# Four residual layers on one NeuronCore: the conv layer's order, the first attention stack and the attention loop are rewritten

## The chip, the cores and the metric

The kernel runs on one core of one Trainium2 chip. The metric is the device time of one launch in microseconds (us). The kernel before was timed three times: 686.96 us in the median, from 685.99 to 689.05. A further execution was profiled, and all rows below are of that one.

## The reference

x is float32, (8, 256, 16, 16): 8 images, 256 channels, 256 positions. Four residual layers follow one another, each behind a group norm of 32 groups of 8 channels.

```
x = x + L0(gn(x)); x = x + L1(gn(x)); x = x + L2(gn(x)); x = x + L3(gn(x))

L0: norm = sqrt(sum_c f*f); fn = f / max(norm, 1e-12)      # f = gn(x)
    corr[r,cc] = sum_c pad(fn)[shifted by r,cc] * fn        # 25 shifts, 5 x 5
    y = relu(conv_w @ concat(f, corr) + conv_b)             # 256 <- 256 + 25
L1: 32 heads of 8 channels; q, k, v = split(x_r @ w_qkv.T + b)
    attn = softmax(q k^T, over the 8 IMAGES); out = attn v
L2: o = gamma * (x x^T)(W x) + x, image by image
L3: 8 experts, the best 2 of each token, gelu(x w1) * (x w3) @ w2
```

In L0 the correlation of two positions p and p' is the product of their unit vectors, which is the same as (f_p . f_p') / (|f_p| |f_p'|).

## The kernel before

A launch handles 2048 tokens (T), in 4 chunks (`NCH`) of 512 columns; a chunk holds 2 images. `x_res` is the residual stream, `x_hat` the normalised one, both with 128 channels on the partitions and 2 halves (`H`). Each engine has one block of code that it runs in order; semaphores tie the engines together. There is no planner: the order is written out by hand in the blocks of SyncE (L258), GpSimd (L350), ScalarE (L403), VectorE (L621) and TensorE (L968).

*Layer L0* goes round chunk by chunk (ScalarE L474 to 490, VectorE L702 to 724, TensorE L1031 to 1046). Of chunk t: `group_norm` sums statistics over groups on TensorE, `variance` (L646, VectorE), `deviation` (L419, ScalarE: ln and exp) and `second_half` (L656, VectorE) make scale and shift; `normalise` (L424, ScalarE) writes the lower half of x_hat and `second_half` the upper one. `squares_of` squares x_hat, `norms` (L985, TensorE) sums the squares over channels with a matrix of ones, `floor_of_norms` (L671) and `power` make 1/norm in `rnorm`, and `unit_vectors` (L675) multiplies x_hat by it into `work`. `gram` (L993) multiplies each tile of 128 tokens with its neighbourhood of 162, `gram_rows` (L442, ScalarE) copies the result out of PSUM, and SyncE writes it to DRAM and reads it back skewed (L278 to 286), which gives a band of shifts per token. `correlations` (L682) picks 25 of them under an edge mask, `turn_correlations` (L1016) transposes them, `turned_correlations` (L454, ScalarE) copies them out, and `conv_correlations` (L1024) adds their product to that of `conv_features` (L1007). `conv_out` (L458) is bias and relu, `add_conv` (L690) adds to x_res, and `statistics(1, ...)` begins the next layer's norm.

*q, k and v* come in 16 tiles: tile n is s = n // 4 (0 and 1: q and k of channels 0 to 127; 2 and 3: of 128 to 255) and chunk c = n % 4. TensorE (L1049) waits for all of L0, then for each tile makes a 128x512 product of q or k in PSUM bank n % 4 and 128 tokens of v. ScalarE (L501) and VectorE (L726) split q and k into three bfloat16 parts, GpSimd (L354) makes the third. SyncE stores the parts to DRAM (`store_parts`, L297), loads the first stack (head 0, i = 0) by six copies straight from SBUF (L305 to 310), then the other three stacks of the group by `load_stack` (L288) from DRAM: one DMA for q and three for k.

*Attention* runs in 8 groups of 4 heads, 16 units each; a unit is a 128 x 128 piece of scores for all 8 images. TensorE makes scores (L1074) and subtracts the maximum over the images (L1083), VectorE takes maximum (L747) and sum (L754), ScalarE exponentials, ln and inverse (L528 to 538), GpSimd multiplies the exponentials by the inverse (L363), and TensorE multiplies with v (L1097). `attention_steps` (L232) writes the steps of TensorE, VectorE and ScalarE: group 0 as straight code, groups 1 to 6 as a loop of two passes with three groups in its body, group 7 and the rest straight. GpSimd and SyncE have loops of their own, one pass a group.

L2 and L3 follow; the change touches them only where a semaphore's count is written (the waits on `gn_var` and the like, which count the calls of the group norm).

## Time and profile before

| | |
|---|---|
| median of three runs | 686.96 us (685.99 to 689.05) |
| the profiled execution | 684.06 us, span 681.9 us |
| TensorE matmul busy | 580.0 us, 85% of the span, 4548 instructions |
| VectorE busy | 476.0 us, 70% |
| GpSimd busy | 383.2 us, 56% |
| ScalarE busy | 327.6 us, 48% |
| chain of waits, by engine | GpSimd 38%, TensorE 35%, "issue" 10%, VectorE 7% |
| mean granted clock of TensorE | 0.896 of 2.4 GHz |

PE is TensorE (PEld its loads of weights), DVE VectorE, ACT ScalarE, POOL GpSimd, SP SyncE; a q behind a name is the engine's sequencer or queue. L363 is line 363 of the kernel before. The chain of waits is followed back from the last instruction: at each step to what released it. "issue" is time in which an engine waited for nothing that the profile shows. A timeline merges instructions of one line: start, duration, engine, line, output<-input, shapes, count, and in brackets the idle time ahead of it and what ended it. A view by stretches gives its bounds and length, then the busy us of five engines with their counts of instructions, the granted clock (1.00 is 2.4 GHz, 0.50 is 1.2 GHz), the mean share of the 16 DMA engines and the GB/s they moved.

### The profile page before, as it was taken

What the parts mean: (1) busy time and instruction counts of PE and PEld (TensorE: products, weight loads), DVE (VectorE), ACT (ScalarE), POOL (GpSimd) and SP (SyncE); (2) the same over time, 40 slices, a digit from 0 to 9 for tenths busy, and PEclk for the clock granted to TensorE, in tenths of its full rate; (3) what the DMA queues carried; (4) which work ended last, traced back from release to release, by engine and by line L of the source; (5) the groups of instructions that cost most, each with busy time, mean ns of one, the idle gap of its engine ahead of it and who ended that gap; (6) DMA issues with size and microseconds to landing.
All of it is one profiled execution on the core that took longest, in us unless ns stands there. A gap on an engine that the chain in (4) does not pass through costs nothing.

```text
span 681.9 us, 13628 instructions
## 1 busy us (share of the span) xinstructions
PE 580.0 (85%) x4548; PEld 367.2 (54%) x4549; DVE 476.0 (70%) x835; ACT 327.6 (48%) x707; POOL 383.2 (56%) x237
## 2 busy tenths in 40 slices
PE   3777795899999997999999999499974799999954
PEld 2444363655555554665555555278863366666633
DVE  3434575799999998699999999566558334334325
ACT  2334466467676765467667676234321133333310
POOL 1000046399999998479999999422001466666520
PEclk9777879699999999589999999789985699999985
DMA  9711115623112221112221100000002223222239
GB/s 303 295 33 32 32 70 149 254 85 104 70 63 70 70 69 68 31 47 71 67 67 60 62 29 1 1 0 1 32 32 65 64 79 95 86 86 92 72 100 309
DMA packets 30520, 56.58 MB, mean 83 GB/s; under 512 B 8362, under 2 KB 22339, under 8 KB 29443
## 3 DMA queue, kind: packets, MB, share of 16 engines
q1 hardware_dynamic: 25715, 38.97, 17.7%
q0 software_dynamic: 3744, 10.39, 4.9%
q10 hardware_dynamic: 1008, 6.49, 2.4%
q8 instruction: 37, 0.61, 0.4%
q14 instruction: 16, 0.13, 0.1%
HBM read 37.84 MB, written 17.40 MB: 81 GB/s over the span
## 4 chain that ended last, share of the span: by engine, by line
POOL 38%; PE 35%; issue 10%; DVE 7%; ACT 4%; DMA 3%; SPq 1%; POOLq 1%; ACTq 0%
POOL e_ring L363 38%; PE ps L1246 10%; PE ps L1262 5%; PE ps L989 2%; PE ps L1057 2%; PE ps L1178 2%; PE ps L1013 2%; DVE stats L639 2%; PE ps L1200 2%; PE ps L1002 1%; PE ps L1136 1%; PE ps L1191 1%; PE ps L1238 1%; SPq L340 1%; PE ps L1254 1%
## 5 line engine op out<-in xcount | busy, mean ns | idle before, releaser
L363 POOL TENSOR_TENSOR e_ring<-e_ring,x_hat 128x1024 f32<-128x1024 f32 x128 | 272.7, 2134 | 47.2 <-ACT x_hat L538 35.9
L528 ACT ACTIVATE e_ring<-ps 128x1024 f32<-128x1024 f32 x128 | 131.2, 1025 | 105.4 <-PE ps L1083 105.4
L747 DVE TENSOR_REDUCE m_bf<-ps 128x128 bf16<-128x1024 f32 x128 | 155.5, 1215 | 16.6 <-PE ps L1074 16.6
L754 DVE TENSOR_REDUCE x_hat<-e_ring 128x128 f32<-128x1024 f32 x128 | 154.8, 1210 | 6.4 <-ACT e_ring L528 6.3
L1074 PE MATMUL ps<-q_stack,k_stack 72*128 72x128 bf16 x1024 | 142.4, 325 | 13.3 <-DMA k_stack<-e_ring 9.7
L1074 PEld LDWEIGHTS ps<-q_stack,k_stack 72*128 72x128 bf16 x1024 | 106.5, 135 | 40.5 <-issue 40.1
L1083 PE MATMUL ps<-m_bf,ident_neg 128*128 128x512 bf16 x256 | 82.5, 406 | 14.1 <-DVE m_bf L747 6.7
L1097 PE MATMUL ps<-e_ring,v_slot 128*32 128x128 f32 x2048 | 87.7, 289 | 3.6 <-POOL e_ring L363 3.6
L1097 PEld LDWEIGHTS ps<-e_ring,v_slot 128*32 128x32 f32 x2048 | 50.9, 110 | 59.8 <-issue 53.4
L1246 PE MATMUL ps<-w_sb,e_ring 128*128 x156 | 75.2, 605 | 0.3 <-issue 0.3
L396 POOL DMA_INDIRECT pair_rows<-scratch,slot_y x39 | 38.5, 987 | 39.4 <-DVE scratch L951 37.6
L357 POOL TENSOR_TENSOR e_ring<-e_ring 128x512 bf16<-128x512 f32 x8 | 9.2, 1158 | 90.8 <-ACT e_ring L499 89.9
L944 DVE TENSOR_TENSOR scratch<-ps,e_ring 128x256 f32<-128x256 f32 x39 | 16.6, 424 | 59.7 <-ACT e_ring L611 59.7
L386 POOL DMA_INDIRECT e_ring<-token_rows,slot_x x39 | 37.9, 972 | 18.6 <-issue 11.6
L1083 PEld LDWEIGHTS ps<-m_bf,ident_neg 128*128 128x128 bf16 x256 | 18.6, 109 | 43.9 <-DVE m_bf L747 43.1
L538 ACT ACTIVATE x_hat<-x_hat 128x128 f32<-128x128 f32 x128 | 39.6, 309 | 4.7
L611 ACT ACTIVATE e_ring<-ps 128x256 f32<-128x256 f32 x39 | 15.0, 384 | 54.9 <-PE ps L1246 54.9
L1262 PE MATMUL ps<-w_sb,scratch 128*128 x156 | 40.3, 381 | 0.4 <-ACT scratch L616 0.4
L532 ACT ACTIVATE x_hat<-x_hat 128x128 f32<-128x128 f32 x128 | 38.5, 301 | 0.7 <-DVE x_hat L754 0.7
L1246 PEld LDWEIGHTS ps<-w_sb,e_ring 128*128 128x128 f32 x156 | 27.2, 194 | 19.9 <-issue 19.9
L606 ACT ACTIVATE e_ring<-ps 128x256 f32<-128x256 f32 x39 | 15.0, 384 | 37.3 <-PE ps L1238 37.3
L375 POOL TENSOR_TENSOR e_ring<-e_ring,tab 128x1248 bf16<-128x1248 bf16 x1 | 2.3, 2276 | 52.6 <-DVE e_ring L896 52.6
(149 smaller groups left out, 702.4 us busy)
## 6 DMA issues: line engine op xcount, KB each, us to landing
q_stack<-qk_parts SPq DMA_DIRECT2D x31, 288.0 KB
k_stack<-qk_parts SPq DMA_DIRECT2D x93, 96.0 KB
w_sb<-in_w13T_dram ACTq DMA_DIRECT2D x2, 2048.0 KB, 10.0
qk_parts<-e_ring SPq DMA_DIRECT2D x2, 1536.0 KB, 5.1
qk_parts<-scratch SPq DMA_DIRECT2D x2, 1536.0 KB, 16.3
x_res<-in_x_dram SPq DMA_DIRECT2D x8, 256.0 KB, 4.0
w_sb<-in_w2T_dram ACTq DMA_DIRECT2D x2, 1024.0 KB, 15.8
token_rows<-work SPq DMA_DIRECT2D x4, 512.0 KB, 3.0
```

Of the source, the lines that this page charges most:

```text
L363: nc.gpsimd.tensor_tensor(ev, ev, view(x_hat, CH + (u % RS) * P, [[0, BQ], [1, P], [0, 2]]), ALU.mult).then_inc(norm_done, 1)
L396: nc.gpsimd.indirect_dma_start(out=y_dram[:, :], in_=y_rows[:, k % YR], in_offset=None, out_offset=bass.IndirectOffsetOnAxis(ap=slot_y[:, ...
L528: nc.scalar.activation(e_ring[:, u % ER, :], score_banks(v), ACT.Exp).then_inc(exp_done, 1)
L532: nc.scalar.activation(s_ln[:, u % 2], s_sum[:, u % 2], ACT.Ln).then_inc(ln_done, 1)
L538: nc.scalar.activation(s_inv[:, u % RS], s_ln[:, u % 2], ACT.Exp, scale=-1.0).then_inc(r_done, 1)
L747: nc.vector.tensor_reduce(m_bf[:, u % 2], by_position(score_banks(v).rearrange("p a c -> p (a c)")), AXY, ALU.max).then_inc(max_done, 1)
L754: nc.vector.tensor_reduce(s_sum[:, u % 2], by_position(e_ring[:, u % ER, :]), AXY, ALU.add).then_inc(sum_done, 1)
L1074: last = nc.tensor.matmul(view(ps, 2 * (v % SLOT) * CH + (b // 2) * (2 * P) + b % 2, [[2, P]]), k_stack[:, i, b * N + mh * P:b * N + (mh + ...
L1083: last = nc.tensor.matmul(bank(2 * (v % SLOT) + j), ident_neg[:], view(m_bf, (u % 2) * P, [[0, BQ // 2], [1, P], [0, 2]]), start=False, st ...
L1097: last = nc.tensor.matmul(ps[32 * (b % 4):32 * (b % 4) + 32, 6, (b // 4) * N + nh * P:(b // 4) * N + (nh + 1) * P], v_slot[:, b * H + mh, ...
L1246: last = nc.tensor.matmul(bank((r + 1) % 2), x_turned[:, (r + 1) % 2, h * P:(h + 1) * P], w13_sb[:, h, bass.ds(e * (2 * C), 2 * C)], start ...
L1262: last = nc.tensor.matmul(ps[:, 6 + (r + 1) % 2, 0:C], gated_t[:, (r + 1) % 2, f * P:(f + 1) * P], w2_sb[:, f, bass.ds(e * C, C)], start=( ...
```

## The change

All of x is normalised first; the correlations are taken from x_hat and multiplied by 1/norm of the one position when the Gram rows leave PSUM (VectorE) and of the other when the turned correlations do. `rnorm` has two buffers. q and k tiles run over lower channels first, chunk by chunk (q and k of chunk 0, of chunk 1, ...), the first eight in two PSUM banks, and five of them are put between the last steps of L0. The first stack is loaded from DRAM as the others. `attention_steps` has no loop. The group norms of chunks 1 to 3 of layer L0 are one call (`variance(0, 1, 3)` and so on).

```diff
         def attention_steps(eng, step):
...
-            with eng.Fori(0, (NG - 2) // SLOT) as t:
-                for j in range(1, SLOT + 1):
-                    for u in range(UPG):
-                        step(t * (SLOT * UPG) + (j * UPG + u), j * UPG + u, u, t * SLOT + j, lambda k: True)
-            for u in range(UPG):
-                step((NG - 1) * UPG + u, (NG - 1) * UPG + u, u, NG - 1, lambda k: True)
+            for U in range(UPG, UNITS):
+                step(U, U, U % UPG, U // UPG, lambda k: True)
...
+        QK_TILES = [(s, c) for half in range(H) for c in range(NCH) for s in (2 * half, 2 * half + 1)]
+        QK_BANK = [2 + n % 2 if n < 2 * NCH else n % 4 for n in range(2 * H * NCH)]
+        TAIL_QK = ((0,), (1, 2), (3, 4))
...
# SyncE
             for s in range(2):
-                sp.wait_ge(part3, NCH * (s + 1))
+                sp.wait_ge(part3, 2 * NCH - 1 + s)
                 store_parts(0, s)
-            for a in range(PARTS):
-                rows_a = slice(a * PARTS * D, (a + 1) * PARTS * D)
-                q_src = parts[0][0:D, 0]
-                k_src = bass.AP(parts[0].tensor, 2 * H * UW + (PARTS + a) * T, [[H * ER * UW, D], [0, PARTS], [1, T]])
-                sp.dma_start(q_stack[rows_a, 0, :], q_src).then_inc(stack_in[0], 16)
-                sp.dma_start(k_stack[rows_a, 0, :], k_src).then_inc(stack_in[0], 16)
             for n in range(2):
                 sp.wait_ge(parts_out[n], 16)
-            for i in range(1, HPG):
+            for i in range(HPG):
                 load_stack(0, i)
...
# ScalarE, the new order of L0 and of the first tiles
+            inverse_norms(0)
+            deviation(0, 1, NCH - 1)
+            for c in range(1, NCH):
+                normalise(0, c)
+                squares_of(c)
+            for t in range(1, NCH):
+                inverse_norms(t)
+                if t >= 2:
+                    deviation(1, t - 2)
+                    normalise(1, t - 2)
+                conv_out(t - 1)
             act.wait_ge(consts_in, 16 * LATER)
+            deviation(1, NCH - 2)
+            normalise(1, NCH - 2)
+            for n in TAIL_QK[0] + TAIL_QK[1]:
+                qk_tile(n)
+            conv_out(NCH - 1)
+            for n in TAIL_QK[2]:
+                qk_tile(n)
+            deviation(1, NCH - 1)
+            normalise(1, NCH - 1)
+            for n in range(5, 2 * H * NCH):
+                qk_tile(n)
...
# VectorE
-            def unit_vectors(c):
...
+            def gram_rows(c):
+                dve.wait_ge(rn_done, c + 1)
...
+                for t in range(TPC):
+                    i, hb = c * TPC + t, t % 2
+                    dve.wait_ge(gram_done, i + 1)
+                    off = GST + (c % 2) * TPC * ROW + t * ROW + (0 if hb else REACH)
+                    q0 = (t // 2) * N + (P - REACH if hb else 0)
+                    nc.vector.tensor_tensor(view(scratch, off, [[1, ROW - REACH]]), ps[:, 2 + i % 2, 0:ROW - REACH],
+                                            rnorm[c % 2][:, q0:q0 + ROW - REACH], ALU.mult).then_inc(gram_row, 1)
+            def turned_correlations(d):
+                dve.wait_ge(cor_tr, d + 1)
+                nc.vector.tensor_tensor(cor_t[:, d * CH:(d + 1) * CH], ps[0:NK, 0, :], rnorm[d % 2][0:NK], ALU.mult
+                                        ).then_inc(cor_t_done, 1)
...
+            for t in range(1, NCH):
+                floor_of_norms(t)
+                if t >= 2:
+                    variance(1, t - 2)
+                correlations(t - 1)
+                if t >= 2:
+                    second_half(1, t - 2)
+                gram_rows(t)
+                turned_correlations(t - 1)
+                add_conv(t - 1)
+                statistics(1, t - 1)
+            dve.wait_ge(consts_in, 16 * LATER)
+            variance(1, NCH - 2)
+            second_half(1, NCH - 2)
+            for n in TAIL_QK[0]:
+                qk_tile(n)
+            correlations(NCH - 1)
+            turned_correlations(NCH - 1)
+            for n in TAIL_QK[1]:
+                qk_tile(n)
+            add_conv(NCH - 1)
+            statistics(1, NCH - 1)
+            for n in TAIL_QK[2]:
+                qk_tile(n)
+            variance(1, NCH - 1)
+            second_half(1, NCH - 1)
+            for n in range(5, 2 * H * NCH):
+                qk_tile(n)
...
# TensorE
+            group_norm(0, 0)
+            conv_features(0, 0)
+            norms(0)
+            group_norm(0, 1, NCH - 1)
+            gram(0)
+            conv_features(0, 1)
+            for t in range(1, NCH):
+                norms(t)
+                if t >= 2:
+                    group_norm(1, t - 2)
+                gram(t)
+                turn_correlations(t - 1)
+                conv_features(t, 0)
+                conv_correlations(t - 1)
+                conv_features(t, 1)
+            group_norm(1, NCH - 2)
+            for n in TAIL_QK[0]:
+                qk_tile(n)
+            turn_correlations(NCH - 1)
+            for n in TAIL_QK[1]:
+                qk_tile(n)
+            conv_correlations(NCH - 1)
+            for n in TAIL_QK[2]:
+                qk_tile(n)
+            group_norm(1, NCH - 1)
+            for n in range(5, 2 * H * NCH):
+                qk_tile(n)
```

`gram` reads x_hat in place of `work` and waits for x_hat alone. `qk_tile` holds what the body of the loop over 16 tiles held, with the bank from `QK_BANK`, and a tile waits for the second tile before it to have left its bank (n < 8), or the fourth.

## Rows read from the trace of the kernel before

**Rows 1.** the page's chain of waits by line, share of the span

```profile
POOL e_ring L363 38%; PE ps L1246 10%; PE ps L1262 5%; PE ps L989 2%; PE ps L1057 2%; PE ps L1178 2%; PE ps L1013 2%; DVE stats L639 2%; PE ps L1200 2%; PE ps L1002 1%; PE ps L1136 1%; PE ps L1191 1%; PE ps L1238 1%; SPq L340 1%; PE ps L1254 1%
```

**Rows 2.** timeline of GpSimd in attention: start us, us, instructions, idle before

```profile
218.44 31.48 POOL L363 TENSOR_TENSOR e_ring<-e_ring,x_hat 128x1024 f32<-128x1024 f32 x14 [0.65 <-ACT x_hat L538]
...
255.16 15.67 POOL L363 TENSOR_TENSOR e_ring<-e_ring,x_hat 128x1024 f32<-128x1024 f32 x7 [0.65 <-ACT x_hat L538]
...
275.77 2.13 POOL L363 TENSOR_TENSOR e_ring<-e_ring,x_hat 128x1024 f32<-128x1024 f32 x1 [4.95 <-ACT x_hat L538]
...
303.92 31.48 POOL L363 TENSOR_TENSOR e_ring<-e_ring,x_hat 128x1024 f32<-128x1024 f32 x14 [0.47 <-ACT x_hat L538]
```

**Rows 3.** timeline of TensorE at the seam of the loop

```profile
265.29 1.05 PE L1074 MATMUL ps<-q_stack,k_stack 72*128 72x128 bf16 x8
...
271.20 1.89 PE L1074 MATMUL ps<-q_stack,k_stack 72*128 72x128 bf16 x8 [3.58 <-issue]
```

**Rows 4.** busy us of PE, PEld, DVE, ACT, POOL; clock, DMA share, GB/s

```profile
270.00:271.00 1.00, 0.00 (x0) 0.00 (x0) 0.00 (x0) 0.00 (x0) 0.82 (x1) 0.50 0.22 86
...
292.00:294.00 2.00, 2.00 (x22) 1.28 (x22) 1.31 (x2) 1.56 (x4) 0.48 (x1) 0.53 0.01 2
```

**Rows 5.** the same view for the time ahead of attention

```profile
11.00:120.00 109.00, 82.95 (x268) 45.70 (x268) 56.14 (x159) 51.79 (x106) 18.45 (x16) 0.83 0.35 117
```

**Rows 6.** timeline of VectorE, the floors of the norms of chunks 1 and 3

```profile
29.41 0.69 DVE L673 TENSOR_SCALAR scratch<-ps 128x512 f32<-128x512 f32 x1 [5.32 <-PE ps L989]
...
65.55 0.69 DVE L673 TENSOR_SCALAR scratch<-ps 128x512 f32<-128x512 f32 x1 [5.44 <-PE ps L989]
```

**Rows 7.** SyncE, TensorE's first scores; GB/s of 95:128 us in 40 slices

```profile
98.72 5.57 SPq L299 DMA_DIRECT2D qk_parts<-e_ring  x2
...
120.71 3.57 PE L1074 MATMUL ps<-q_stack,k_stack 72*128 72x128 bf16 x16 [9.69 <-DMA k_stack<-e_ring]
...
GB/s 0 0 0 20 0 238 477 477 343 372 0 194 298 462 477 462 70 45 60 40 45 55 60 55 50 50 55 50 50 60 70 129 159 129 139 119 129 109 144 253
```

**Rows 8.** VectorE's lines ahead of attention by form: count | busy us, mean ns

```profile
L731 DVE SCALAR_TENSOR_TENSOR e_ring<-ps,qk_bias_sb,scratch 128x512 f32<-128x512 f32 x8 | 6.0, 750 | 1.8 <-ACT scratch L504 1.8
...
L735 DVE TENSOR_TENSOR work<-ps,v_bias_sb 128x256 f32<-128x256 f32 x16 | 6.6, 413 | 0.0
...
L693 DVE TENSOR_TENSOR x_res<-x_res,scratch 128x1024 f32<-128x1024 f32 x4 | 4.9, 1217 | 1.5 <-ACT scratch L465 1.5
...
L639 DVE BATCH_NORM_STATS2 stats<-x_res 128x6 f32<-128x256 f32 x32 | 11.2, 414 | 5.0 <-DMA x_res<-in_x_dram 4.9
...
L660 DVE SCALAR_TENSOR_TENSOR gn_tmp<-gn 128x4 f32<-128x4 f32 x8 | 1.3, 163 | 7.3 <-ACT gn L417 7.3
```

**Rows 9.** SyncE, first band's read; the four reads, us to landing

```profile
30.61 0.37 SPq L285 DMA_DIRECT2D scratch<-gram_rows  x1
...
scratch<-gram_rows SPq DMA_DIRECT2D x4, 138.0 KB, 2.3
```

**Rows 10.** timeline of ScalarE: ln of the norms, the last normalisation

```profile
48.31 0.63 ACT L416 ACTIVATE scratch<-scratch 128x512 f32<-128x512 f32 x1 [3.75 <-DVE scratch L673]
...
91.50 1.09 ACT L429 ACTIVATE x_hat<-x_res,gn 128x256 f32<-128x256 f32 x2 [0.82 <-DVE gn L663]
```

**Rows 11.** timeline of TensorE: features, correlations' product cold and warm

```profile
48.06 3.71 PE L1013 MATMUL ps<-x_hat,conv_wT_sb 128*128 128x512 f32 x8
...
58.27 3.73 PE L1027 MATMUL ps<-e_ring,conv_cT_sb 25*128 25x512 f32 x4 [3.42 <-ACT e_ring L456]
...
72.65 1.98 PE L1027 MATMUL ps<-e_ring,conv_cT_sb 25*128 25x512 f32 x4 [0.33 <-ACT e_ring L456]
```

**Rows 12.** timeline of GpSimd, the first eight tiles of q and k

```profile
93.83 10.08 POOL L357 TENSOR_TENSOR e_ring<-e_ring 128x512 bf16<-128x512 f32 x8 [89.94 <-ACT e_ring L499]
```

**Rows 13.** SyncE, a load of q; GB/s of 174:184 us in 40 slices

```profile
174.95 0.77 SPq L291 DMA_DIRECT2D q_stack<-qk_parts  x1
...
GB/s 98 66 82 82 49 33 16 33 0 66 49 0 49 49 115 131 131 213 131 98 115 164 82 197 147 82 82 49 82 82 66 98 49 82 16 0 0 0 0 0
```

More of the change, by code:

```diff
@@ L119, in conv_stack_kernel @@
         TPC = CH // P
-        rnorm = scratch[:, 0:CH]
-        GST = CH
+        rnorm = [scratch[:, i * CH:(i + 1) * CH] for i in range(2)]
+        GST = 2 * CH
         BAND = GST + 2 * TPC * ROW
@@ L353, in _ @@
             pool.wait_ge(pool_init, 2)
-            for n in range(2 * H * NCH):
-                s, c = n // NCH, n % NCH
+            for n, (s, c) in enumerate(QK_TILES):
                 pool.wait_ge(part2, n + 1)
@@ L1009, in conv_features @@
                     pe.wait_ge(conv_in, 16 * CONV)
+                normed(0, BPC * (d + 1) - 1)
                 if d >= 2:
```

240 lines of the change are left out of this document (92 added, 148 removed).

## The prediction

> **What bounds the kernel now.** I read the page's chain of waits first, then GpSimd's timeline through attention, then the first 121 us engine by engine, then the queue of SyncE around the first scores. The chain shows that the longest stretch hangs on one GpSimd instruction, the multiplication of the exponentials on L363: 38% of the span, and most of it is this one line [rows 1]; eight groups of sixteen units make 128 of them. They follow one another every 2.26 us (14 of them take 31.48 us, each 2.13 us long), and one group of sixteen units lasts 255.16 - 218.44 = 36.72 us [rows 2]. While GpSimd is the bound, nothing that the change does to the other engines inside attention counts, with one exception. Between the same place of two groups there are once 303.92 - 255.16 = 48.76 us, 12.04 us more than 36.72 [rows 2]. That place is the seam between the first and the second pass of the loop in the function attention_steps: GpSimd, which has a loop of its own by groups, stands still for 4.95 us, and before it TensorE for 3.58 us, on nothing that the profile shows ("issue") [rows 2, 3]. Then TensorE's granted clock is 0.50 (the 1.2 GHz level) and is still 0.53 some 22 us later [rows 4]; the eight score matmuls of a unit take 1.89 us instead of 1.05 [rows 3]. So the seam costs 12.0 us: the stall itself and the slow clock behind it.
>
> Ahead of attention no engine is full. TensorE's clock was 0.83 in the mean from 11 to 120 us, and it was busy for 83 of the 109 us [rows 5]. The chunks go round a chain through all three engines, from one floor of the norms to the next: 18 us for the last two of them, (65.55 - 29.41) / 2 [rows 6]. The first scores begin at 120.71, after 9.69 us of waiting for the first stack [rows 7].
>
> **Part 1, the straight loop.** It takes out the jump back of TensorE, VectorE and ScalarE. The 64 units ahead of the seam are straight code already, 16 before the loop and 48 in its first pass, and the two groups' starts in [rows 2] that lie there are the steady 36.72 us apart. With every unit written out I expect that pace throughout: -12.0 us. Bounds: nothing is gained if the stall is merely met elsewhere; more than 12.04 us can't be, as that is all the seam costs. I take the upper end, as it is what the row shows of straight code.
>
> The Trainium skill, on the page "Runtime: NRT & Kernel Launch", section "Instruction fetch mechanics", says that instructions are prefetched in sequence and that a taken jump to code outside the small buffer has to wait for a fetch from memory. By that rule the stall goes, as in my sum; the trace agrees with it in the 3.58 us [rows 3].
>
> **Part 2, the conv layer.** Removed: the unit vectors (one 128x1024 multiplication per chunk) from the chain, and the normalisation and squares of a chunk from between two chunks. Added: each 128x162 row copy goes from ScalarE to VectorE and becomes a product with the norms; no row has it. Its shapes lie below 128x256 (413 ns) and 128x512 (750 ns) of the same kind [rows 8]; on the line through both, 162 columns come to 0.29 us. Bounds 0.2 and 0.41 us; four per chunk, so at most 0.5 us a chunk later. The turned correlations, 512 columns, I take at 0.75 us, the nearest row, between 0.4 and 0.75.
>
> I lay the new order out by these lengths. *First chunk*: x_hat at 11.0 as before; the features, now ahead of the norms, cost what the unit vectors gave, and I put its four rows at 20.5. Normalising the rest follows in 7 us. VectorE then stands in order before the correlations of chunk 0, and these wait for the band. Its read was issued at 30.61 and such a read lands in 2.3 us [rows 9]. The write ahead of it shares the DMA engines with the weights' 6 MB, issued in the same place as before, so writing the rows a little earlier doesn't help, and the band is there at 32.9. From there: correlations, rows of chunk 1 (with TensorE cold after 5 us of idling) to 36.1, turned 37.7, features and correlations product to about 41, relu, addition, statistics (0.7 + 1.22 + 1.8 us, the last four of 414 ns [rows 8] and two small ones) to 44.8. The floor of chunk 2 is thus at 44.8 instead of 47.6.
>
> *From one floor to the next*, warm, in us after the floor begins: floor 0.7 [rows 6]; inverse norms (two of 0.63 [rows 10]) 2.0; deviation 2.45; second half (four small ones of about 0.2 with their gaps, two 128x256 of some 0.4 [rows 8]) 4.0; rows, two waiting for their Gram matmuls, 5.9; turning 6.2; turned correlations 6.95, beside them features on TensorE to 7.75 (two pairs take 3.71 [rows 11]); correlations' product 1.7 [rows 11], 9.45; relu 10.15; addition 11.4; statistics 13.2. Cold, features and product take 3.4 and 3.4 (the product 3.73 against 1.98 with its pipeline's end [rows 11]): 16.6. The transfer of the rows lies beside all this. So 13.2 to 16.6 us in place of 18.
>
> *The tail.* Behind the last statistics of chunk 2 the new order sets in one line on VectorE: group norm 3.4, tile 0 to 5.6, correlations and turned of chunk 3 to 7.25, tiles 1 and 2 to 10.4, product, relu, addition and statistics of chunk 3 to 14.45, tiles 3 and 4 (1.1 us each [rows 8]) 16.65, group norm and x_hat 19.8 (1.09 us at the end as in [rows 10]); tiles 5 to 7, and 25.9 until GpSimd has the third part of the eighth tile. TensorE idles in it for over 2 us before turning chunk 3, so cold it is 2 to 4 us more. The moved tiles hide little: correlations of chunk 3, ready since its band came, now stand behind tile 0.
>
> Sum to the eighth tile: all warm 44.8 + 13.2 + 13.2 + 25.9 = 97.1; all cold 44.8 + 33.2 + 29.5 = 107.5. It was 103.9 (93.83 + 10.08 [rows 12]). The middle is 102.3, and the mean clock of 0.83 [rows 5] lies between the two levels; I take 102.5, 1.4 us earlier. The tiles behind the eighth run at TensorE's 1.3 us as before and end 7 us later, ahead of the stack.
>
> **Part 3, the first stack by DRAM.** Six copies from SBUF go, ahead of which nothing of the stack can land; the scores began at 120.71, 16.8 us after the eighth tile [rows 7, 12]. Now the two stores of 1.57 MB leave 1.3 us apart. The first alone fills five slices of 0.825 us behind its issue at 98.72 (238 to 477 GB/s, 4.1 us) [rows 7]; both at 430 GB/s are 7.3 us, begun 0.9 us ahead of the eighth tile, so with the landing they are there 6.9 us behind it (5.7 at the best slices' rate, 7.8 at the first store's). One issue of q and three of k follow; the traffic of such a load, issued at 174.95, ends in the 35th of 40 slices of 0.25 us, at 182.9, or 8.0 us later [rows 13]. So the scores may begin 6.9 + 0.1 + 8.0 = 15.0 us after the eighth tile: -1.8 us. Bounds: 6.5 us for the load, as its tail may be that of others (-3.3), and 11 us, as three more loads follow at once (+1.2). The second stack follows by 6 us, and unit 4 needs it only some 9 us after the start. TensorE idles 8 us in either, so the cold start of attention, 8.7 us to GpSimd's first product, stays.
>
> The Trainium skill ("DMA: Bandwidth & Descriptors", the section on why a DMA increments its semaphore by 16) says that the slowest dimension of a pattern sets how many of the 16 engines share a DMA. The load of q leads with a dimension of three copies; by the rule three engines carry all 288 KB. The slices with a long tail at about 82 GB/s [rows 13] agree; by it there is no 6.5 us, and the sum would be the same 8.0.
>
> **Sum.** Scores begin at 102.5 + 15.0 = 117.5 against 120.7: -3.2. With the seam -12.0: -15.2 us. What follows attention has the same instructions in the same order. The profiled execution took 684.06 us (span 681.9 and 2.2 around it): 668.9. The median of the runs, 686.96, lies 2.9 above; from it 671.8. I say 671.5.
>
> **Rivals.** *B, the clock holds up front (0.15)*: eighth tile 97.1, scores 112.1, -8.6; with -12.0 a time of 666. For it: TensorE's longest gap in a chunk shrinks from 3.4 us [rows 11] to about 2.6. Against: the clock was 0.83 with TensorE busy for 76% of the time [rows 5], and in the new order that share hardly rises.
> *C, the new order is slower up front (0.15)*: all cold, eighth tile 107.5, scores 122.5, +1.8; 677. VectorE now carries rows, turned correlations and tiles in one order; each late band or stall holds all behind it.
> *D, one stall stays (0.05)*: if the supply of instructions stalls once in the longer straight code, it costs the 12.04 us again: 684. The seam may be a matter of distance and not of the jump. Against it speak 64 units without one.
> *E, slower (0.05)*: the same mechanism, in attention, met twice or more, since 48 more units have to be fetched by three engines while the stacks load: each stall with its slow clock is 12.04 us, so with two the time is 671.8 + 24.1 = 696. It decides from the second stall on.
> *Mine, A*: 0.60.
>
> **How the numbers follow.** About 0.5% (3.4 us) is what a measurement can tell from no change. A, B and C are faster: 0.90; D is within: 0.05; E slower: 0.05. The range leaves out D, E and the edges of B and C: 663 to 679, from -24 (B with the better stack) to -8 (C with the worse stack).
>
> **What would show it.** Right: GpSimd's products 2.26 us apart from start to end, each group 36.7 us, no clock of 0.50 inside attention; floors of chunks 2 and 3 near 44.8 and 60; the eighth tile near 102.5; scores 15 us later with TensorE waiting for a k_stack from qk_parts. Wrong: a stall on "issue" inside attention, first scores before 112 or after 123, or floors over 18 us apart. If the part behind attention changes by more than 1 us, the sum has missed something.

## The result, and the profile of the changed kernel

The changed kernel takes 679.88 us (median of 10 runs, 676.09 to 682.86) against 687.61 us of the kernel before (10 runs, 683.09 to 698.43): ratio 0.9887, 95% interval 0.9855 to 0.9920. It is 7.7 us faster, where the prediction had 15.2. Its profiled execution took 682.86 us, the longest of its ten, and the one of before 684.06, shorter than its median; so the two profiles lie only 1.2 us apart and the stages have to be compared one by one. Ratios, here and below, are estimated from fast runs alone, which leaves out runs far above the fastest of their kernel (one of the six of s2 below took 933.11 us, at a mean clock of 0.555), while the medians are of all runs.

*Attention.* GpSimd's timeline of the changed kernel, where [rows 2] shows the seam:

```profile
219.94 31.48 POOL L361 TENSOR_TENSOR e_ring<-e_ring,x_hat 128x1024 f32<-128x1024 f32 x14 [0.65 <-ACT x_hat L530]
251.77 4.23 POOL L361 TENSOR_TENSOR e_ring<-e_ring,x_hat 128x1024 f32<-128x1024 f32 x2 [0.35 <-ACT x_hat L530]
256.65 31.48 POOL L361 TENSOR_TENSOR e_ring<-e_ring,x_hat 128x1024 f32<-128x1024 f32 x14 [0.65 <-ACT x_hat L530]
288.49 4.23 POOL L361 TENSOR_TENSOR e_ring<-e_ring,x_hat 128x1024 f32<-128x1024 f32 x2 [0.36 <-ACT x_hat L530]
```

From one group's place to the next there are 256.65 - 219.94 = 36.71 us, across the former seam as everywhere else; no idle time of 4.95 us, and no clock of 0.50 from 138 us until attention ends. Its last product ends at 423.52 us, against 434.07 before: 10.55 us sooner.

*Ahead of attention.* Floors of chunks 1 to 3 on VectorE; the eighth tile on GpSimd; SyncE's stores of lower q and k and its first loads; TensorE's first scores:

```profile
25.83 0.69 DVE L667 TENSOR_SCALAR scratch<-ps 128x512 f32<-128x512 f32 x1 [2.23 <-PE ps L1008]
45.01 0.69 DVE L667 TENSOR_SCALAR scratch<-ps 128x512 f32<-128x512 f32 x1
59.89 0.68 DVE L667 TENSOR_SCALAR scratch<-ps 128x512 f32<-128x512 f32 x1
...
102.14 1.15 POOL L355 TENSOR_TENSOR e_ring<-e_ring 128x512 bf16<-128x512 f32 x1 [0.82 <-ACT e_ring L465]
...
101.34 2.33 SPq L304 DMA_DIRECT2D qk_parts<-e_ring  x2
110.68 0.91 SPq L296 DMA_DIRECT2D q_stack<-qk_parts  x1
111.64 1.42 SPq L300 DMA_DIRECT2D k_stack<-qk_parts  x2
...
120.79 3.57 PE L1106 MATMUL ps<-q_stack,k_stack 72*128 72x128 bf16 x16 [10.39 <-DMA k_stack<-qk_parts]
```

The floors are where the prediction put them (45.01 and 59.89 for 44.8 and 60; [rows 6] had 65.55 for the last). The eighth tile's third part is there at 102.14 + 1.15 = 103.29 us, 0.6 us sooner than in [rows 12], and then 17.5 us pass to the first scores (16.8 before, 15.0 in the sum): 120.79 against the 120.71 of [rows 7]. Of the 5.7 us that the last floor gained nothing is left: from that floor to the eighth tile there are 103.29 - 59.89 = 43.4 us, where the old order needed 103.91 - 65.55 = 38.4 (the prediction had 42.5).

*Start of attention.* The view by stretches, first of before and then of the changed kernel:

```profile
120.00:130.00 10.00, 9.29 (x38) 7.60 (x39) 6.02 (x6) 2.56 (x4) 0.63 (x1) 0.50 0.58 202
130.00:140.00 10.00, 8.70 (x96) 5.40 (x95) 9.83 (x10) 7.26 (x14) 9.55 (x5) 1.00 0.62 258
```

```profile
120.00:130.00 10.00, 9.21 (x38) 7.63 (x39) 5.93 (x5) 2.56 (x4) 0.55 (x1) 0.50 0.74 292
130.00:140.00 10.00, 10.00 (x72) 7.40 (x71) 8.80 (x9) 6.05 (x12) 7.96 (x4) 0.62 0.35 146
```

With the same start, TensorE is at full clock from 130 us before and gets 0.62 in the mean of 130 to 140 us now: GpSimd has 4 products behind it in that stretch instead of 5.

*Behind attention* nothing was changed, but from the end of attention to the end of the span there are 680.7 - 423.52 = 257.2 us instead of 681.9 - 434.07 = 247.8. Two stages carry it. The first lies between the addition to x_res and the product with the tables on GpSimd, 77.76 us before (443.97 to 521.73) and 81.05 now:

```profile
433.01 2.49 POOL L370 TENSOR_TENSOR x_res<-x_res,x_hat 128x512 f32<-128x512 f32 x2 [9.49 <-ACT x_hat L427]
...
514.06 2.28 POOL L373 TENSOR_TENSOR e_ring<-e_ring,tab 128x1248 bf16<-128x1248 bf16 x1 [53.43 <-DVE e_ring L916]
```

The second is the 39 expert slots, whose results GpSimd writes one by one to pair_rows: 111.65 us from the first to the last of them before (every 3.02 us in the steady part), 657.33 - 539.03 = 118.30 us now. It limps, that is, short and long steps take turns:

```profile
566.64 0.99 POOL L394 DMA_INDIRECT pair_rows<-scratch,slot_y  x1 [0.30 <-DVE scratch L958]
569.25 0.99 POOL L394 DMA_INDIRECT pair_rows<-scratch,slot_y  x1 [0.34 <-issue]
574.32 0.99 POOL L394 DMA_INDIRECT pair_rows<-scratch,slot_y  x1 [2.80 <-DVE scratch L971]
576.92 0.99 POOL L394 DMA_INDIRECT pair_rows<-scratch,slot_y  x1 [0.34 <-issue]
...
571.30 0.39 ACT L598 ACTIVATE e_ring<-ps 128x256 f32<-128x256 f32 x1 [3.24 <-remote]
```

The steps are 2.6, 5.1 and 2.6 us long, and at a long one ScalarE stood still for 3.24 us, until 571.30, though TensorE's product for it had ended at 568.67. So there were four questions: what the loop was worth, what the conv order, what the stack, and whether the part behind attention belongs to the change.

### The profile page after: what moved, and what is told of

The parts are those of the page before. It is cut to its first block, busy times and chain, and to the rows that moved or that the text cites. A ratio compares the mean times of both kernels' runs of the same rounds, so it can differ in the third digit from the quotient of the medians.

```text
span 680.7 us, 13220 instructions
## 1 busy us (share of the span) xinstructions
PE 573.0 (84%) x4540; PEld 363.3 (53%) x4541; DVE 474.5 (70%) x835; ACT 320.2 (47%) x683; POOL 383.5 (56%) x237
## 4 chain that ended last, share of the span: by engine, by line
POOL 38%; PE 32%; DVE 9%; issue 9%; DMA 4%; ACT 4%; another core or an unknown queue 1%; SPq 1%; POOLq 1%; ACTq 0%; DVEq 0%
POOL e_ring L361 38%; PE ps L1278 9%; PE ps L1294 5%; DVE stats L631 2%; PE ps L1061 2%; PE ps L1232 2%; PE ps L1210 2%; PE ps L1032 1%; PE ps L1168 1%; PE ps L1270 1%; DMA gram_rows<-scratch 1%; PE ps L1223 1%; PE ps L1286 1%; PE ps L1021 1%
## 5 line engine op out<-in xcount | busy, mean ns | idle before, releaser
L1106 PE MATMUL ps<-q_stack,k_stack 72*128 72x128 bf16 x1024 | 139.5, 320 | 10.4 <-DMA k_stack<-qk_parts 10.4
L1106 PEld LDWEIGHTS ps<-q_stack,k_stack 72*128 72x128 bf16 x1024 | 104.4, 133 | 36.9 <-issue 36.8
L1115 PE MATMUL ps<-m_bf,ident_neg 128*128 128x512 bf16 x256 | 80.4, 397 | 13.4 <-DVE m_bf L767 5.8
L1129 PE MATMUL ps<-e_ring,v_slot 128*32 128x128 f32 x2048 | 85.2, 283 | 3.6 <-POOL e_ring L361 3.6
L598 ACT ACTIVATE e_ring<-ps 128x256 f32<-128x256 f32 x39 | 15.0, 385 | 43.4 <-PE ps L1270 31.5
## 6 DMA issues: line engine op xcount, KB each, us to landing
w_sb<-in_w13T_dram ACTq DMA_DIRECT2D x2, 2048.0 KB, 10.1
w_sb<-in_w2T_dram ACTq DMA_DIRECT2D x2, 1024.0 KB, 15.7
```

The costliest lines, as they stand in the source:

```text
L1106: last = nc.tensor.matmul(view(ps, 2 * (v % SLOT) * CH + (b // 2) * (2 * P) + b % 2, [[2, P]]), k_stack[:, i, b * N + mh * P:b * N + (mh + ...
L1115: last = nc.tensor.matmul(bank(2 * (v % SLOT) + j), ident_neg[:], view(m_bf, (u % 2) * P, [[0, BQ // 2], [1, P], [0, 2]]), start=False, st ...
L1129: last = nc.tensor.matmul(ps[32 * (b % 4):32 * (b % 4) + 32, 6, (b // 4) * N + nh * P:(b // 4) * N + (nh + 1) * P], v_slot[:, b * H + mh, ...
```

## The experiments

Every ratio is to the kernel before, timed on the same chip in the same job. The jobs were r1 to r4, s1 to s4, t1 to t4, u1 to u4, v1 and v2; the kernel before had medians of 685.54, 681.91, 689.41, 685.60 and 688.57 us in them, so times of different jobs are not compared.

**First job: the parts of the change.** r1 is the changed kernel again.

> The changed kernel once more, unaltered: is the slow slot loop of its first profile (39 slots from 539.0 to 657.3 us, 118.3 us, where the kernel before needed 111.7) a property of the program or of that one execution? Theory P (the program: its longer straight code puts the slot loop elsewhere, and ScalarE stalls in it): the slot loop takes about 118 us again and the median stays near 680. Theory E (the execution): the slot loop takes about 112 us and the profiled time is near 676, the lowest of the ten runs.

r2 is the kernel before with the loop of `attention_steps` written out, and nothing else:

```diff
-            with eng.Fori(0, (NG - 2) // SLOT) as t:
-                for j in range(1, SLOT + 1): ...
-            for u in range(UPG): ...
+            for U in range(UPG, UNITS):
+                step(U, U, U % UPG, U // UPG, lambda k: True)
```

> The kernel before with the attention loop written out and nothing else. By the prediction's own step the seam's 12.0 us go: 675.5 from 687.6. Theory P: the straight code costs some 6 us in the slot loop, so about 681. Theory E: 675 to 676, and all that is missing from the forecast is the front part, which then is worth nothing or a loss.

r3 is the changed kernel with that loop put back (the same diff, read backwards).

> The changed kernel with the attention loop of before put back; conv order, tile order and the first stack stay as changed. By the prediction: 684.4, 3.2 us under the kernel before. By the two profiles (scores begin at 120.79 against 120.71): 687 to 689, no gain. Theory P: the slot loop is at 112 us again here; the seam shows its 12 us.

r4 is the changed kernel with the loop of `slot_steps` written out too:

```diff
-            for s in range(7):
-                step(s, s, inside)
-            with eng.Fori(0, (SLOTS - 7) // XR) as i: ...
+            for s in range(SLOTS):
+                step(s, s % XR, inside)
```

> The changed kernel with the loop over the expert slots written out too (32 slots of straight code on TensorE, ScalarE and VectorE in place of 4 passes of 8). Theory P: the stalls of ScalarE in the slot loop (3.2 us at 571, 3.7 us at 609) come with the loop at its place in the code; they go, slot after slot at 3.02 us, and the time is near 674. Theory E: no difference to the changed kernel within 2 us.

| | median us (n) | ratio, 95% interval | attention: first product to end | slots |
|---|---|---|---|---|
| r1 changed | 676.99 (6) | 0.9868 [0.9827, 0.9910] | 129.27 to 422.80 | 113.91 |
| r2 loop alone | 678.21 (6) | 0.9892 [0.9845, 0.9938] | 128.31 to 420.89 | 115.96 |
| r3 loop back | 686.09 (12) | 1.0011 [0.9981, 1.0041] | 132.69 to 432.57 | 113.20 |
| r4 slots straight | 677.17 (6) | 0.9871 [0.9821, 0.9922] | 132.93 to 432.43 | 111.65 |

The loop alone is worth all that the change is worth; conv order and stack together are worth 1.0011, nothing. The slots of r1 and the time of r2 lie between what the theories P and E had. r4 has the even slots of theory P and the time of theory E: in its profile the clock stays at 0.50 until 155 us, and attention lasts 299.5 us. r3 shows that the seam's price is not a constant. Its timeline of GpSimd there:

```profile
261.03 15.67 POOL L365 TENSOR_TENSOR e_ring<-e_ring,x_hat 128x1024 f32<-128x1024 f32 x7 [0.65 <-ACT x_hat L534]
281.92 15.27 POOL L365 TENSOR_TENSOR e_ring<-e_ring,x_hat 128x1024 f32<-128x1024 f32 x7 [5.22 <-ACT x_hat L534]
297.55 4.23 POOL L365 TENSOR_TENSOR e_ring<-e_ring,x_hat 128x1024 f32<-128x1024 f32 x2 [0.35 <-ACT x_hat L534]
```

The same stall (5.22 us, against 4.95 in [rows 2]), but behind it no product is late, since TensorE's clock was back at 1.00 before 282 us; the loss is 4.7 us and not 12.

**Second job: each part by itself, and before once more.** s1 is the kernel before, unaltered.

> The kernel before, nothing changed, profiled once more. Theory 1 (the profile on which the 12 us of the seam rest was one execution whose clock fell at the seam; another execution has the stall without the fall): TensorE's last score product before the seam to the first behind it again 3 to 5 us, but the next group's first GpSimd product 41 to 49 us after the last group's, instead of 36.7 us; ratio 1.000 +- 0.003. Rival (the fall of the clock follows the stall every time in this kernel): 48.8 us again, as before. On the slot loop: theory 1a (its stalls belong to every kernel with a loop of 8 slots): 113 to 118 us from the first to the last expert product on GpSimd, not the 111.65 us of the first profile; rival (they come with the changed kernel's code): 111.7 us again.

s2 is before with both loops written out (both diffs above).

> The kernel before with both the attention loop and the slot loop written out; conv order and first stack as before. Theory 1 (two loops, two separate prices): attention's gain of 7 us (r2) and 2 to 6 us of the slot loop, which has 111.7 us: ratio 0.983 to 0.987. Rival (what the slot loop gives up comes back as a lower TensorE clock or another stall, as the equal medians of r1 and r4 suggest): ratio 0.987 to 0.991, the same as with the attention loop alone.

s3 is before with the first stack by DRAM:

```diff
-            for a in range(PARTS):
-                ... six copies from parts[0] to q_stack and k_stack ...
-            for i in range(1, HPG):
+            for i in range(HPG):
                 load_stack(0, i)
```

> The kernel before with only the first stack read back from DRAM. Theory 1 (after the 8th tile's last part the stores land in about 7.4 us and the load takes 10.1 us, against 16.8 us now, and every stack of the first group comes with it): scores start 0 to 2 us later, ratio 1.000 to 1.003. Rival (the six reads out of SBUF also hold up the stores; without them the stack is there sooner, as predicted): scores 1.5 to 3 us earlier, ratio 0.996 to 0.998.

s4 is the changed kernel with the loop and those six copies put back, so the conv order alone.

> The kernel before with only the conv layer's new order: x all normalised first, correlations scaled as they leave PSUM, q and k lower channels first; first stack from SBUF, both loops kept. Theory 1 (the 8th tile is there only 0.6 us sooner, and the front gives nothing): scores at 119 to 121 us, ratio 0.998 to 1.001. Rival (the conv order alone is worth the 1.4 us that the sum gave it, and the stack took it back): scores 1 to 2 us earlier than 120.7, ratio 0.996 to 0.998.

| | median us (n) | ratio, 95% interval | 8th tile, first scores | attention | slots |
|---|---|---|---|---|---|
| s1 before | 680.12 (12) | 0.9984 [0.9947, 1.0022] | 103.21, 120.09 | 128.76 to 429.27 | 111.69 |
| s2 both loops | 675.51 (6) | 0.9900 [0.9852, 0.9947] | 103.21, 120.09 | 128.75 to 421.35 | 111.75 |
| s3 stack | 678.77 (12) | 0.9969 [0.9937, 1.0001] | 104.67, 120.31 | 128.97 to 425.58 | 111.68 |
| s4 conv order | 682.07 (12) | 1.0011 [0.9979, 1.0043] | 103.99, 122.69 | 131.34 to 432.52 | 111.65 |

Theory 1 of s1 holds in its number: in one more profile of the same kernel the seam's group lasts 44.6 us (254.52 to 299.11) instead of 48.76, and attention 300.5 us instead of 304.7. But the clock falls here too, only for a shorter time. GpSimd in s1, behind the seam:

```profile
275.06 2.12 POOL L363 TENSOR_TENSOR e_ring<-e_ring,x_hat 128x1024 f32<-128x1024 f32 x1 [4.88 <-ACT x_hat L538]
278.75 2.12 POOL L363 TENSOR_TENSOR e_ring<-e_ring,x_hat 128x1024 f32<-128x1024 f32 x1 [1.56 <-ACT x_hat L538]
282.43 2.13 POOL L363 TENSOR_TENSOR e_ring<-e_ring,x_hat 128x1024 f32<-128x1024 f32 x1 [1.56 <-ACT x_hat L538]
285.46 6.32 POOL L363 TENSOR_TENSOR e_ring<-e_ring,x_hat 128x1024 f32<-128x1024 f32 x3 [0.89 <-ACT x_hat L538]
```

Two gaps of 3.7 us follow, at half clock, where the first profile had five. s3, by DRAM, has 15.6 us from the eighth tile to the scores, near the prediction's 15.0, but its eighth tile is late, at 104.67, so the scores begin no sooner than in s1: its ratio is the rival's, its start nearer to theory 1's. s4 has theory 1's ratio, but its scores lie outside both ranges: the conv order alone brings the eighth tile no sooner and the scores 2.6 us later than in s1. No kernel of this job limps in the slots, with or without the slot loop: theory 1a of s1 falls, and s2, whose ratio is its rival's, says little on that loop.

**Third job.** t1 asks whether the lower clock at the start of attention is what the front's gain went into:

```diff
             pe.wait_ge(rest_done, 2 * H * NCH)
+            pe.wait_ge(v_stored, 2 * H * NCH)
+            for _ in range(10):
+                nc.tensor.matmul(bank(7), ones_sb[:], conv_wT_sb[:].rearrange("p h o -> p (h o)"), start=True, stop=True)
             attention_steps(pe, attention_step)
```

> The changed kernel with ten matmuls of constants into a free bank between the last q and k tile and the first scores, where TensorE is idle for 10.4 us and its clock falls to half; nothing of the computation changes. Theory 1 (the new conv order leaves TensorE's clock low for 16 to 34 us after the first scores, against 6 to 9 us with the old order, and this takes back what the front could have given): the clock stays at full speed into attention, the first GpSimd product comes 2 to 3 us sooner than 129.5 us and the units are 2.6 us apart from the start; 3 to 6 us sooner in all, ratio to before 0.980 to 0.984 where the changed kernel has 0.988. Rival (the clock falls in any case within the first units, or the load of the stack sets the start and the rest is hidden): within 1 us of the changed kernel, ratio 0.986 to 0.990.

t2 is s3 with both loops written out, t3 is t2 with t1's matmuls.

> The kernel before with the first stack by DRAM and both the attention loop and the slot loop written out; the old conv order stays. Theory 1 (the stack by DRAM is worth 0.3%, the attention loop 1.1%, and the prices add): ratio 0.985 to 0.988. Rival (the 0.3% of the stack alone was scatter): ratio 0.989 to 0.991, as with both loops written out alone.

> The same as t2 with the ten matmuls of constants in the gap before the first scores. Theory 1 (with the old conv order the clock is low for only 6 to 9 us after the first scores, and keeping it up is worth half of that): 2 to 4 us sooner than t2, ratio 0.980 to 0.984. Rival (the clock falls somewhere else instead, for as long): same as t2 within 1 us.

t4 is r3 with one more wait on ScalarE.

```diff
                 elif U == 2:
+                    act.wait_ge(stack_in[0], 16)
```

> The kernel r3 (the changed kernel with the attention loop restored), which stalls in the slot loop, with one more wait on ScalarE ahead of the loop, on a count that has long been reached: ScalarE's instructions then stand where they stand in s4, which did not stall. Theory 1 (whether a pass of the slot loop stalls hangs on where ScalarE's instructions stand in memory): 111.6 to 111.8 us from the first to the last expert product and no interval over 3.3 us between two of them. Rival (it stalls for another reason, such as the DRAM loads of the stack or the state of that execution): 113 us again.

| | median us (n) | ratio, 95% interval | first scores | attention | slots |
|---|---|---|---|---|---|
| t1 | 680.73 (6) | 0.9862 [0.9805, 0.9919] | 118.96 | 125.01 to 420.35 | 116.69 |
| t2 | 673.21 (6) | 0.9773 [0.9718, 0.9828] | 119.80 | 128.46 to 420.86 | 114.75 |
| t3 | 676.79 (6) | 0.9783 [0.9719, 0.9847] | 120.21 | 126.25 to 424.93 | 112.81 |
| t4 | 685.38 (1) | (none) | 120.22 | 128.88 to 426.34 | 116.53 |

The matmuls (each shows as two instructions) do what they should to the clock and nothing for the time. TensorE in t1, and the stretches behind it:

```profile
109.09 8.82 PE L1157 MATMUL ps<-conv_wT_sb,ones_sb 128*128 128x512 f32 x20 [1.54 <-DVE work L715]
118.96 1.92 PE L1106 MATMUL ps<-q_stack,k_stack 72*128 72x128 bf16 x16 [1.05 <-DMA k_stack<-qk_parts]
```

```profile
120.00:128.00 8.00, 5.46 (x41) 3.73 (x39) 7.33 (x7) 4.17 (x7) 2.40 (x2) 1.00 0.79 312
128.00:136.00 8.00, 7.22 (x57) 4.30 (x56) 6.76 (x7) 4.32 (x9) 6.10 (x3) 0.61 0.45 183
```

Sixteen score matmuls take 1.92 us instead of 3.57, the first product comes at 125.01, and then the clock is at 0.50 from 129.8 to 136.6 us: attention needs 295.3 us from its first product, more than the 292.7 to 294.1 of the changed kernel's three profiles. t3 is the same (0.50 from 128.8 to 145.9 us; 298.7 us against 292.4 in t2). The rivals were right: the clock falls elsewhere instead. t2's ratio lies below both of its ranges.

t4 and t2 end the theories on the slots so far. t4 limps although its added wait puts ScalarE's code where it stands in s4, and t2 limps with its slots written out; all four kernels of this job do, on another chip than the second job's, where none did. But three of the four of the first job did as well, and those ran on the second job's chip.

**Fourth job: what was left open.** u1 is before, u2 the changed kernel, u3 is s3 with the attention loop written out (the changed kernel but for the conv order), u4 is t2 again.

> The kernel before, one more profile, on the chip on which u2 to u4 run. Theory 1 (the stalls in the slot stage belong to the chip and the hour): its slot stage shows them if u2 does and not if u2 does not, 113 to 118 us or 111.7 us in both. Rival (they belong to the changed kernel and its like): 111.7 us here and 113 to 118 us in u2. Seam: 4 to 8 us over 36.7, not 12.

> The changed kernel, beside u3 and u4. Theory 1 (the conv order gives nothing and leaves TensorE's clock low for longer behind the first scores): ratio 0.986 to 0.990, 2 to 4 us slower than u3. Rival (the conv order is neutral): the same as u3 within 1 us.

> The changed kernel with the old conv order: only the first stack by DRAM and the attention loop written out. Theory 1 (the old conv order lets the clock return 6 to 9 us behind the first scores, not 16 to 30): ratio 0.980 to 0.985, 2 to 4 us faster than u2. Rival (conv order neutral): 0.986 to 0.990 as u2.

> u3 with the slot loop written out as well, which is t2 once more. Theory 1 (the slot loop has no price of its own, since t2 stalled with its slots written out): same as u3 within 1 us, ratio 0.980 to 0.985. Rival (it has one): 2 to 4 us faster than u3, ratio 0.975 to 0.979.

| | median us (n) | ratio, 95% interval | 8th tile, first scores | attention | slots |
|---|---|---|---|---|---|
| u1 before | 690.08 (1) | (none) | 103.55, 120.25 | 128.91 to 433.39 | 118.08 |
| u2 changed | 680.27 (6) | 0.9886 [0.9829, 0.9942] | 103.24, 120.82 | 129.48 to 422.15 | 117.49 |
| u3 | 676.39 (6) | 0.9875 [0.9819, 0.9931] | 103.84, 118.71 | 127.37 to 420.68 | 117.00 |
| u4 | 675.52 (6) | 0.9841 [0.9782, 0.9900] | 104.29, 119.88 | 128.54 to 420.94 | 115.85 |

The kernel before limps here as the changed one does. GpSimd in u1:

```profile
570.36 0.99 POOL L396 DMA_INDIRECT pair_rows<-scratch,slot_y  x1 [1.57 <-DVE scratch L951]
572.92 0.99 POOL L396 DMA_INDIRECT pair_rows<-scratch,slot_y  x1 [0.30 <-DVE scratch L938]
576.89 0.99 POOL L396 DMA_INDIRECT pair_rows<-scratch,slot_y  x1 [1.70 <-DVE scratch L951]
579.46 0.99 POOL L396 DMA_INDIRECT pair_rows<-scratch,slot_y  x1 [0.30 <-issue]
```

Steps of 2.6 and 4.0 us, and 118.08 us in all. So the limp belongs to both kernels: the rival of u1 falls, and the 6.65 us that the first pair of profiles shows in the slots need not be the change's. The seam of u1 costs 11.8 us, though, where I had expected 4 to 8. u2 and u3 differ in the conv order alone, and their ratios are the same within their intervals: it gives nothing, and whether it costs 1 or 4 us these runs can't tell. Nor can u3 and u4 tell whether the slot loop has a price. Theory 1 of u2 and u3, that the new order leaves the clock low for longer, fails here; u2 first, then u3:

```profile
130.00:132.00 2.00, 1.90 (x14) 1.22 (x13) 1.83 (x3) 1.58 (x4) 1.60 (x1) 0.96 0.99 416
```

```profile
130.00:132.00 2.00, 2.00 (x9) 1.53 (x8) 1.79 (x3) 1.15 (x2) 2.00 (x1) 0.50 0.25 102
132.00:134.00 2.00, 2.00 (x23) 0.96 (x22) 2.00 (x2) 0.97 (x3) 1.56 (x2) 0.69 0.25 92
```

The clock is back about 9 us behind the first scores in u2, with the new order, and about 14 us behind them in u3, with the old one.

**Fifth job.** v1 asks why the scores come 17.5 us after the eighth tile in the changed kernel and 15.6 in s3. SyncE's queue in s3, then the traffic of 94 to 120 us in 40 slices of 0.65 us, of s3 and of the changed kernel:

```profile
99.47 5.57 SPq L299 DMA_DIRECT2D qk_parts<-e_ring  x2
109.89 0.92 SPq L291 DMA_DIRECT2D q_stack<-qk_parts  x1
...
GB/s 0 0 0 0 0 0 0 0 0 309 302 492 378 302 605 19 19 321 302 454 454 302 605 0 0 13 0 19 57 126 170 158 132 139 120 151 69 139 107 126
```

```profile
GB/s 0 0 0 0 0 0 0 0 25 0 0 0 302 302 605 302 435 473 303 605 302 454 454 302 13 0 0 0 19 57 107 158 158 113 145 139 120 132 95 139
```

With the old tile order the store of q has gone by when the one of k starts, at the eighth tile (99.47 + 5.57 - 0.35 = 104.69): two humps of six slices, and the load is issued 5.2 us after it. With the new one, q is complete only at the seventh tile, and both stores make one hump of twelve slices that ends at 109.6 us; the load is issued 7.4 us after the eighth tile. v1 cuts the stores of the changed kernel in two:

```diff
-            for s in range(2):
-                sp.wait_ge(part3, 2 * NCH - 1 + s)
-                store_parts(0, s)
+            for t0, t1, first in ((0, T - CH, 2 * NCH - 3), (T - CH, T, 2 * NCH - 1)):
+                for s in range(2):
+                    sp.wait_ge(part3, first + s)
+                    sp.dma_start(... columns t0 to t1 of part s ...).then_inc(parts_out[s], 16)
```

> The changed kernel with each of the two stores of lower q and k parts cut in two: the first three quarters of the columns go out after the 5th and 6th tile, the last quarter after the 7th and 8th. Theory 1 (with q and k tiles in turn both whole stores start within 2 us of each other at the end and land 7.4 to 8 us after the 8th tile, against 5.2 us where only one is left, s3 and u3): the load of the first stack is issued 3 to 5 us after the 8th tile and scores start 2.5 to 4 us sooner, at 116.5 to 118.5 us; ratio 0.982 to 0.986. Rival (the landing is the latency of a store and not its bytes, or the earlier stores slow the q and k tiles): the load is issued 6 us or more after the 8th tile, ratio 0.986 to 0.990 as the changed kernel.

> The fastest version a third time (t2 0.977, u4 0.984). Theory 1 (it is faster than the changed kernel): ratio 0.977 to 0.985. Rival (its 0.977 was scatter, and it equals the changed kernel): 0.986 to 0.990.

v1: 674.00 us (6 runs), ratio 0.9792 [0.9746, 0.9837]; v2: 670.22 us (6 runs), ratio 0.9745 [0.9692, 0.9799]. In v1's profile the first store leaves at 95.52, but the load of the stack only at 106.88, 7.3 us after the eighth tile, as without the cut: my theory fails in its main number, and the ratio lies below both ranges. The bytes explain it: from the fifth tile to the eighth there are 4 us, and 3.1 MB at the 350 to 410 GB/s of its slices need 8 to 9. The scores come 17.0 us after the eighth tile. That they begin at 116.52 is due to the eighth tile, at 99.54 us in this execution. The cut isn't the cause of that: t1, whose stores are whole, has the tile at 100.45, and in both the mean clock was 0.93 from 11 to 60 us and 0.96 from 60 to 99.5, against 0.90 and 0.92 in the first profile of the changed kernel. If the 0.979 is more than such a front's luck, these runs don't show why. In the slots v1 limps (115.48 us) and v2, which is t2 and u4 again, does not (111.75): theory 1 of u1, chip and hour, isn't the whole either, as both ran on one chip.

The lowest ratios are those of before with the first stack by DRAM and both loops written out, 0.9773, 0.9841 and 0.9745 in three jobs, against 0.9887, 0.9868 and 0.9886 of the changed kernel. v2's lies below its own range of 0.977 to 0.985. That this version is faster than the changed kernel is likely but not shown: the two ran side by side in one job only (u4, u2), and their intervals overlap there, as those of v2 and v1 do. Nor do the profiles show a stage that gives it 1% over s2 (0.9900).

## Why the prediction was wrong

**The straight loop (-12.0 us): right in mechanism, mis-sized.** The stall and its clock are gone as predicted. But the 12.04 us were one execution's. From the first product to the end, attention lasts 292.4 to 293.3 us in the six executions with the old conv order, the loop written out and no added matmuls (r2, s2, t2, u3, u4, v2; mean 292.7), and 304.7, 300.5 and 304.5 in the three of the kernel before (first profile, s1, u1): the seam costs 12.0, 7.9 and 11.8 us, 10.6 in the mean. In s3, which keeps the loop too, it costs 4.0, and with it the mean is 8.9. The stall itself is 4.6 to 5.0 us of GpSimd's time in all four; what differs is how long TensorE stays at 1.2 GHz behind it, 24 us in the first profile and 3.4 in s3. My bounds said that more than 12.04 us can't be gained and took the upper end; a price that hangs on the clock has bounds of its own, 4 and 12 us. By medians, r2 gained 7.4 us [4.3, 10.6].

Measured from one group's place to the next, as in [rows 2], the seven executions with the loop fall into two sets: 12.0, 7.9, 11.8 and 7.7 us where the first stack comes from SBUF (before, s1, u1, s4), and 4.2, 4.7 and 5.1 where it comes by DRAM (s3, r3, t4). So part of what looks like scatter may belong to the kernel, and part of what the stack seems to give in s3 may be a cheaper seam; no run was made to test that.

The Trainium skill, page "Runtime: NRT & Kernel Launch", section "Instruction fetch mechanics", says that a taken branch to a target outside the prefetched pages stalls until the target has been fetched. r2 against before agrees, since the stall of 4.95 us goes with the jump alone; that the time is spent on fetching, no view shows.

**The conv layer (-1.4 us to the eighth tile): -0.4 us.** Floors, row products (0.32 us for 0.29) and turned correlations (0.68 for 0.75) came as laid out. The eighth tile is at 103.29, 102.82 and 103.24 us (changed kernel, r1, u2) against 103.91, 103.21 and 103.55 (before, s1, u1). Over all executions it comes at 99.5 to 107.4 us in the nine of the new order (mean 103.4) and at 102.8 to 105.2 in the eleven of the old one (mean 103.8). So both edges of the prediction, 97.1 all warm and 107.5 all cold, were nearly met: early in v1 and t1, at the clocks given above, late in r4 and r3 (107.4 and 106.3), with 0.86 and 0.91 in the same two stretches.

**The first stack (-1.8 us): the step that failed in the sum.** The 15.0 us from the eighth tile to the scores were 6.9 to the landing of both stores, 0.1, and 8.0 for the load. The changed kernel needs 17.5, 17.8 and 17.6 us. The landing takes 7.4, 8.0 and 8.0: in the first profile the traffic runs from 102 to 109.6 us, and the load is issued 1.1 us behind its end. The load, priced after a single one in attention (whose row ends after 7.8 us, not 8.0), takes 9.6 to 10.1 us; three more are issued right behind it, which is the reason that the prediction gave for its bound of 11, but no run has the load without them. With the old order of tiles the stack by DRAM gives 15.6, 14.9, 15.7, 15.6 and 14.9 us (s3, u3, t2, u4, v2) against 16.7 to 16.9 from SBUF. That this is near 15.0 is luck: it is 5.2 to 6.1 us to the landing, since one store has gone by, and 9.5 to 10.4 for the load. The new order of tiles takes this gain back, as both stores end together. With the stack from SBUF the new order is worse still, 18.7 us (s4). The Trainium skill ("DMA: Bandwidth & Descriptors", why a DMA increments its semaphore by 16) says that the slowest dimension of a pattern sets how many engines share it. The slices behind the load's issue, 57 to 170 GB/s against 302 to 605 of the stores ahead of it, don't speak against it, but the loads of k run in them too, so they don't show how many engines carry q.

**The start of attention, which I said stays:** it doesn't always. Without added matmuls the first stretch of 2 us at full clock starts at 128 to 134 us in the ten executions of the old order; in the eight of the new one at 128 (t4), 132 (u2), 134 (v1) and at 138 to 156 in the other five. The attention of the changed kernel lasts 294.1, 293.5 and 292.7 us, and 299.5 in r4, against the 292.7 above: 0 to 7 us more. Five of eight are late, but the two sets overlap, and u2 and u3 stand the other way round, so that the new order is the cause isn't shown; t1 shows only that filling the gap doesn't bring the time back.

**Behind attention** the first pair differs by 9.3 us, and the prediction had said that over 1 us there means something missed. What it had missed is how far one kernel's executions differ: the stage from the addition to the tables takes either 77.7 to 77.8 us or 80.9 to 81.5, in kernels of both sorts (before 77.76, s1 81.48; t1 77.75, the changed kernel 81.05), and the slots take 111.7 to 118.3 us, 111.65, 111.69 and 118.08 in the kernel before (first profile, s1, u1). From the end of attention to the end of the span the kernel before has 247.8, 251.4 and 254.4 us and the changed one 257.2, 252.7 and 257.2: 4.5 more in the mean. The values overlap; whether chance alone makes the difference isn't shown.

Together, from three executions of each kernel: -10.6 for the seam, +0.4 for the first scores ((120.79 + 120.60 + 120.82 - 120.71 - 120.09 - 120.25) / 3), +0.7 for the clock behind them ((1.4 + 0.8 + 0.0) / 3) is -9.5 us, and -5.0 with the 4.5 behind attention; the medians have -7.7, with an interval from -10.0 to -5.5. So the forecast of -15.2 was short in two terms above all: the seam by 1.4 us, or 3.1 with s3 counted in, and the front by 3.6, of which 2.6 are the stack's and 1.0 the conv layer's.

The range ended at 679 because it took one execution's seam as a constant. Its edges don't follow from its own bounds either: C with the worse stack is 107.5 + 18.0 = 125.5 us for the scores, +4.8, so -7.2 in all and 679.8, and B with the better one is -22.1, not -24. Rivals: C came nearest in place and sign (front slower), but by the stack and not by a late eighth tile, and it wasn't enough alone; B's warm front came in t1 and v1 alone; D and E didn't occur.

## What to carry to other kernels

A stall's price read from one profile is the price in one execution; where TensorE's clock falls behind it, take a second profile of the same kernel before the sum takes it at full size, and compare stages that the change doesn't touch to see how far two profiles of one kernel differ. A loop whose body is passed twice can be worth 1% when it is written out. Work moved ahead of a transfer must not also move the end of the transfer's other half: here two stores that end together land 7.4 to 8.0 us behind the last tile, and the second by itself 5.2 to 6.1.

## What was unexpected of the hardware

The slot stage ran evenly at 3.02 us a slot in some executions and in steps of 2.6 and 4 to 5 us in others of the same kernel, up to 6.4 us longer in all; no view names the cause, and neither the loop (t2, u4 limp without it) nor where ScalarE's code stands (t4) is it. Ten matmuls that keep TensorE at full clock through a gap of 10 us moved the fall of the clock to 129.8 us in t1, behind a stretch in which TensorE was busy for 5.46 of 8 us, and to 128.8 in t3, and gained nothing. With the loop, the same seam left TensorE at half clock for anything from 3.4 to 24 us.
